# Two experts per row instead of eight: rows gathered by expert behind an attention layer

## The reference

```python
def xattn(latents, context, Wq, Wk, Wv, Wo):       # 16 heads, 4 key/value heads of 96
    hidden = concatenate([context, latents], axis=1)
    q, k, v = latents @ Wq.T, hidden @ Wk.T, hidden @ Wv.T     # by heads
    attn = softmax(q k^T / sqrt(96))
    return (attn v) @ Wo.T
def ffn(x, W_gate, b_gate, W_e, b_e):
    _, top_idx = top_k(x @ W_gate + b_gate, 2)
    y_all = relu(einsum('bsd,edh->bseh', x, W_e) + b_e)        # 8 experts
    return take_along_axis(y_all, top_idx[..., None], axis=2).mean(axis=2)
x = x + xattn(layernorm(x), ctx, Wq, Wk, Wv, Wo)
x = x + ffn(layernorm(x), W_gate, b_gate, W_e, b_e)
```

## Time and profile before

| | |
|---|---|
| median of 3 runs | 3558.59 us (3557.27 to 3558.87) |
| the profiled execution | 3555.37 us; its span from first to last instruction 3553.6 us |
| TensorE (PE) | 3503.6 us busy, 99% of the span, 22132 passes |
| VectorE (DVE) | 2121.9 us, 60% |
| ScalarE (ACT) | 1706.8 us, 48% |
| GpSimd (POOL) | 893.4 us, 25% |
| DMA | 262.34 MB, mean 74 GB/s |
| granted clock of TensorE | 0.996 of full speed over the span |
| chain that ended last, by its largest share | L1404 on TensorE, 8% |

### The profile page before, as it was taken

One profiled execution on the slowest core, in us unless ns is written; L12 is line 12 of the kernel. 1 busy time (PEld: TensorE's weight loads), 2 busy tenths in 40 slices (PEclk: granted clock), 3 DMA queues, 4 the chain that ended last, 5 costly groups with the idle time before them and its releaser, 6 DMA issues. The chain is left out here.

```text
span 3553.6 us, 65357 instructions
## 1 busy us (share of the span) xinstructions
PE 3503.6 (99%) x22132; PEld 3228.6 (91%) x22132; DVE 2121.9 (60%) x3055; ACT 1706.8 (48%) x3204; POOL 893.4 (25%) x692
## 2 busy tenths in 40 slices
PE   8999999999999999999999999999999999898999
PEld 8989999999999999999999999999999999887887
DVE  5356666666666666666666666666666666555554
ACT  3235555555555555555555555555555555423222
POOL 0042222222222222222222222222222222400000
PEclk9999999999999999999999999999999999999999
DMA  6532222222222222222222222222222222363110
GB/s 229 201 120 62 62 62 62 62 62 62 62 62 62 62 60 60 61 62 62 62 62 62 62 60 59 61 62 62 61 59 60 61 62 62 93 192 114 36 36 33
DMA packets 301138, 262.34 MB, mean 74 GB/s; under 512 B 198690, under 2 KB 255394, under 8 KB 300466
## 3 DMA queue, kind: packets, MB, share of 16 engines
q1 hardware_dynamic: 301106, 261.94, 24.9%
HBM read 195.50 MB, written 66.35 MB: 74 GB/s over the span
## 5 line engine op out<-in xcount | busy, mean ns | idle before, releaser
L812 PE MATMUL ps_proj<-wv_hi,parts 128*125 128x384 f32 x3072 | 875.1, 339 | 0.0
L757 DVE TENSOR_TENSOR probs_lo<-probs,probs_hi 125x448 fp32r<-125x448 f32 (+1 forms) x896 | 679.9, 775 | 275.5 <-ACT probs_hi L684 263.1
L799 PE MATMUL ps_proj<-parts,wk_hi 128*128 128x500 f32 x2304 | 709.7, 389 | 2.9 <-DVEq L712 2.9
L812 PEld LDWEIGHTS ps_proj<-wv_hi,parts 128*125 128x125 f32 x3072 | 560.0, 186 | 4.7
L676 ACT ACTIVATE probs<-ps_scores 125x448 f32<-125x448 f32 (+1 forms) x896 | 463.0, 517 | 116.4 <-PE ps_scores L860 73.4
L812 PE MATMUL ps_proj<-wv_lo,parts 128*125 128x384 f32 x1536 | 518.4, 337 | 0.0
L799 PEld LDWEIGHTS ps_proj<-parts,wk_hi 128*128 128x128 f32 x2304 | 430.7, 188 | 90.9 <-DVEq L712 3.2
L663 ACT CAST values_hi<-ps_proj 125x384 fp32r<-125x384 f32 x384 | 184.5, 480 | 661.9 <-PE ps_proj L812 661.9
L684 ACT CAST probs_hi<-probs 125x448 fp32r<-125x448 f32 (+1 forms) x896 | 484.1, 540 | 28.3
L134 POOL TENSOR_SCALAR parts<-raw 128x1000 fp32r<-128x1000 f32 (+1 forms) x198 | 239.4, 1209 | 968.8 <-PE ps_proj L812 790.2
L726 DVE TENSOR_TENSOR values_lo<-ps_proj,values_hi 125x384 fp32r<-125x384 f32 x384 | 214.2, 558 | 430.1 <-ACT values_hi L663 428.1
(11 more groups left out here) (159 smaller groups left out, 6115.0 us busy)
## 6 DMA issues: line engine op xcount, KB each, us to landing
raw<-in_ctx SPq DMA_DIRECT2D x192, 500.0 KB, 3.6
qk_hi<-proj_out_hi SPq DMA_DIRECT2D x60, 224.0 KB, 2.0
qk_lo<-proj_out_lo SPq DMA_DIRECT2D x60, 224.0 KB, 2.4
queries_hi<-qk_hi SPq DMA_DIRECT2D x32, 336.0 KB, 3.5
queries_lo<-qk_lo SPq DMA_DIRECT2D x32, 336.0 KB, 3.6
att_raw<-attended SPq DMA_DIRECT2D x128, 84.0 KB
probs<-att_raw SPq DMA_DIRECT2D x31, 336.0 KB, 5.6
probs<-inverse_sums SPq DMA_DIRECT2D x31, 336.0 KB, 3.0
```

The costliest lines, as they stand in the source:

```text
L757: dve.tensor_tensor(prs[1][0:R, u % PRING, 0:N], pr[0:R, u % PRING, 0:N], f(prs[0][0:R, u % PRING, 0:N]), ALU.subtract).then_inc(p_lo, 1)
L799: mm = pe.matmul(pproj[n % 2][:, 0:CS], w["wk"][a][:, j // 3, i * P:(i + 1) * P], ct[v][:, c, j // 3, :], start=(j == 0), stop=(j == 3 * K ...
L812: mm = pe.matmul(pproj[n % 2][0:VT, 0:KD], ct[a][:, t // VTC, j // 3, s], w["wv"][v][:, j // 3, :], start=(j == 0), stop=(j == 3 * KT - 1))
```

## The change

Each row goes to its two experts only. In **combine**, gate writes for each row two one-hot rows (`sels`) of the chosen experts. A matrix product with a triangle of ones counts, for each row, how many rows of its tile ahead of it chose the same expert, and one with a matrix of ones adds those of all tiles before (rank). VectorE's put makes of it a place in a list (expert x 1792 + rank), and GpSimd writes the row's number to that place in DRAM by an indirect DMA, two for each tile (scatter). GpSimd also splits five eighths of every expert's weights, and rows and normed rows are stored to DRAM untransposed.

In **experts**, a table of 35 tiles of 128 places is worked out: for each tile its expert and where its part of the list lies. 35 is the number that suffices for any choice of the experts; all 35 are always computed. The list is gathered (one indirect DMA), turned, and then for each tile GpSimd gathers 128 normed rows by their numbers; TensorE turns them, ScalarE and VectorE split them, and TensorE multiplies by the weights of the tile's expert, whose number it reads from SBUF into a register. One tile's product has 15 passes, as one of the four blocks of rows lies in two homes: nine of 512 columns and six of 256. VectorE adds the bias chosen by its own register, ScalarE applies relu and 0.5, SP stores the tile to DRAM. When all are stored, each tile of 128 rows gathers its two results by indirect DMA, and VectorE adds both to the rows.

In **attend**, the maxima are spread otherwise over the value tiles, and row_max, turn and place_max move.

The core of the diff:

```diff
+NT = (2 * ROWS + E * (P - 1)) // P
+EARLY_W, LATE_W = 2 * D + D // 2, D // 2 + D
+LATE_RING, LO_PIECES = 4, 4
+XRING, X1_RAW = 3, 6
+PIECES = ((0, 0, 0, 0, D), (1, 0, D, 0, D), (2, 0, 2 * D, 0, D // 2), (2, 1, 0, D // 2, D), (3, 1, D // 2, 0, D))
 def value_parts(t):
-    first = (CHUNKS - 1) * KTILES + 2 * t
-    return first, first + 1
+    first = (CHUNKS - 1) * KTILES
+    return (first + max(2 * t - 1, 0), first + 2 * t if 0 < t < READY - 1 else PARTS)
...
                         if t == READY - 1:
+                            row_max(b)
+                        if t == READY:
                             place_max(b)
                         values(b, t)
-                        if p < PARTS:
+                        if last < PARTS:
                             part_max(b, last)
-                        if last + 1 == PARTS:
-                            row_max(b)
...
-                        if t == READY - 1:
-                            turn_max(b)
+                            if (t, part) == (READY, 0):
+                                turn_max(b)
...
# combine, SP
+                def load_expert(e):
+                    if e >= 2:
+                        sp.wait_ge(e_lo, e - 1)
+                    sp.dma_start(w_raw[:, e % 2], io["we"][:, e, 0:EARLY_W]).then_inc(e_loaded[e % 2], 16)
+                def store_rows(t):
+                    sp.wait_ge(x1_done, t + 1)
+                    sp.dma_start(scratch["x1"][t], x1[:, t % 2]).then_inc(x1_stored[t % 2], 16)
+                    sp.wait_ge(normed, t + 1)
+                    sp.dma_start(scratch["xn"][t * P:(t + 1) * P], xn[:]).then_inc(xn_stored, 16)
...
# combine, GpSimd
+                def split_expert(e):
...
+                    pool.tensor_scalar(hi, raw, 1.0, 0.0, ALU.mult, ALU.add).then_inc(e_hi, 1)
+                    pool.wait_ge(e_hi, e + 1)
+                    n = EARLY_W // LO_PIECES
+                    for i in range(LO_PIECES):
+                        c = slice(i * n, (i + 1) * n)
+                        op = pool.tensor_tensor(lo[:, c], raw[:, c], f(hi[:, c]), ALU.subtract)
+                    op.then_inc(e_lo, 1)
+                def scatter(t):
+                    pool.wait_ge(placed, t + 1)
+                    for n in range(2):
+                        pool.indirect_dma_start(out=scratch["ids"], out_offset=bass.IndirectOffsetOnAxis(pos[:, t, n:n + 1], 0),
+                                                in_=ids[:, t:t + 1], in_offset=None).then_inc(scattered, 16)
...
# combine, VectorE: put(t - 2) stands ahead of gate(t - 1)
+                def put(t):
+                    dve.wait_ge(ranked, t + 1)
+                    dve.tensor_tensor(place[:], pr[:], base[:], ALU.add).then_inc(place_ready, 1)
...
+                    dve.tensor_copy(pos[:, t, :], spots[:, t, :]).then_inc(placed, 1)
+                    dve.tensor_tensor(cum[:], cum[:], tot[:], ALU.add).then_inc(cum_ready, 1)
# combine, TensorE: rank(t - 2) six passes before the end of output(t)
+                def rank(t):
+                    pe.wait_ge(tot_ready, t + 1)
+                    pe.matmul(pr[:], upper[:], tot[:], start=True, stop=False)
+                    pe.wait_ge(cum_ready, START + t)
+                    pe.matmul(pr[:], allones[:], cum[:], start=False, stop=True).then_inc(ranked, 1)
...
# experts, SP
+                for j in range(NT):
+                    sp.wait_ge(relu_done, j + 1)
+                    sp.dma_start(scratch["y"][j * P:(j + 1) * P], y[:, j % XRING]).then_inc(y_stored[j % XRING], 16)
...
# experts, GpSimd
+                pool.wait_ge(row_ready, 1)
+                pool.wait_ge(early["scattered"], 32 * OT)
+                pool.indirect_dma_start(out=id_rows[:], out_offset=None, in_=scratch["ids"].rearrange("(j p) c -> j (p c)", p=P),
+                                        in_offset=bass.IndirectOffsetOnAxis(id_row[:], 0)).then_inc(ids_loaded, 16)
+                pool.wait_ge(index_done, 1)
+                for j in range(NT):
+                    if j >= XRING:
+                        pool.wait_ge(turned, j - XRING + 1)
+                    pool.indirect_dma_start(out=xg[:, j % XRING], out_offset=None, in_=scratch["xn"],
+                                            in_offset=bass.IndirectOffsetOnAxis(index[:, j:j + 1], 0)).then_inc(gathered[j % XRING], 16)
...
+                for t in range(OT):
+                    s = t % XRING
+                    if t >= XRING:
+                        pool.wait_ge(added, t - XRING + 1)
+                    for n, dst in enumerate((xg[:, s], y[:, s])):
+                        pool.indirect_dma_start(out=dst, out_offset=None, in_=scratch["y"],
+                                                in_offset=bass.IndirectOffsetOnAxis(y_pos[:, t, n:n + 1], 0)).then_inc(y_gathered[s], 16)
# experts, VectorE
+                for j in range(NT):
+                    e = dve.value_load(expert_i[0:1, j:j + 1], min_val=0, max_val=E - 1)
+                    if j + 1 < NT:
+                        lo(j + 1)
...
+                    dve.tensor_tensor(y[:, s], po[s][:], bias[:, bass.ds(e, 1), :].rearrange("p e d -> p (e d)"), ALU.add).then_inc(biased, 1)
# experts, TensorE
+                def product(j, e):
+                    pe.wait_ge(x_lo, j + 1)
+                    if j >= XRING:
+                        pe.wait_ge(biased, j - XRING + 1)
+                    for i, (k, home, c, d0, d1) in enumerate(PIECES):
+                        w = (we_early, we_late)[home]
+                        for a, v in TERMS:
+                            mm = pe.matmul(po[j % XRING][:, d0:d1], xs[a][:, j % XRING, k, :],
+                                           w[v][:, bass.ds(e, 1), c:c + d1 - d0].rearrange("p e d -> p (e d)"),
...
+                for j in range(2):
+                    turn(j)
+                pe.wait_ge(early["late_lo"], E)
+                for j in range(NT):
+                    e = pe.value_load(expert_i[0:1, j:j + 1], min_val=0, max_val=E - 1)
+                    product(j, e)
+                    if j + 2 < NT:
+                        turn(j + 2)
```

More of the change, by code:

```diff
@@ new lines, in _ @@
+                invert_sums(dve, stream, B - 1)
+                split(1)
+                dve.wait_ge(b_hi, 1)
+                dve.tensor_tensor(be_lo.bitcast(F32R), be_raw, f(be[0:E, :]), ALU.subtract).then_inc(b_lo, 1)
+                dve.wait_ge(consts, 14)
+                for t in range(OT - 1):
+                    norm(t)
+                    if t + 2 < OT:
+                        split(t + 2)
+                    if t > 1:
+                        put(t - 2)
+                    if t > 0:
+                        gate(t - 1)
@@ L1162, in _ @@
+                put(OT - 3)
+                gate(OT - 2)
+                norm(OT - 1)
+                put(OT - 2)
+                gate(OT - 1)
+                put(OT - 1)
             @block.tensor
@@ new lines, in experts @@
+        of_j = sb("of_j", [1, NT, E], I32)
+        over, tiles = sb("over", [P, E, SLOTS]), sb("tiles", [P, E])
+        pairs, ends = sb("pairs", [P, E, E]), sb("ends", [P, E])
+        shift, moved, move = sb("shift", [P, E]), sb("moved", [P, 2 * OT, E]), sb("move", [P, 2 * OT])
+        y_pos = sb("y_places", [P, OT, 2], U32)
+        sels, spots, base = (early[n] for n in ("selected", "spots", "bases"))
+        past, before = (x1_more[0:1, 2 + i, 0:NT * E].rearrange("p (j e) -> p j e", e=E) for i in range(2))
@@ L1384, in _ @@
-                for s in range(2):
-                    tile(0, s, True, first=(s == 0))
-                with dve.Fori(1, OT // 2 - 1) as i:
-                    for s in range(2):
-                        tile(i, s, True)
-                for s in range(2):
-                    tile(OT // 2 - 1, s, s == 0)
+                dve.wait_ge(consts, 7)
+                dve.tensor_copy(pick[:], pick_f[:]).then_inc(consts, 1)
+                dve.wait_ge(counted, 1)
+                dve.tensor_tensor(over[:], pcnt.unsqueeze(2).broadcast_to([P, E, SLOTS]), of_m[:], ALU.is_gt).then_inc(table, 1)
@@ L1416, in _, with spread_bias, turn @@
-                for s in range(2):
-                    tile(0, s, first=(s == 0))
-                with pe.Fori(1, OT // 2) as i:
-                    for s in range(2):
-                        tile(i, s)
+                def spread_bias(n):
+                    if n >= 2:
+                        pe.wait_ge(bias_ready, n - 1)
+                    pe.matmul(pb[n % 2][:], pick[:, n, :], be[:], start=True, stop=True).then_inc(spread, 1)
+                def turn(j):
+                    pe.wait_ge(gathered[j % XRING], 16 * (j // XRING) + 16)
+                    if j >= 2:
+                        pe.wait_ge(x_lo, j - 1)
+                    for k in range(KT):
+                        mm = pe.transpose(pt[j % 2][:, k, :], xg[:, j % XRING, k * P:(k + 1) * P], ident[:])
+                    mm.then_inc(turned, 1)
@@ new lines, in _ @@
+                pe.wait_ge(early["cum_ready"], START + OT)
```

(9 more changed lines are left out.)

602 lines of the change are left out of this document (302 added, 300 removed).

## The result

The changed kernel takes 3432.13 us (median of 4 runs, 3431.87 to 3433.05) against 3558.73 us for the kernel before on the same chip; the ratio is 0.9644, with a 95% interval of 0.9627 to 0.9661. The forecast was 3445, in a range of 3405 to 3520. The profiled execution has a span of 3430.3 us, 123.3 less than before.

A forecast was written before the change was run, and what follows sets the result against it. TensorE was taken to bound both long stages. Attend -14.0, combine +11.9 and last stage -109.2 (211.6 against 320.8) took the span from 3553.6 to 3442.3; 1.8 around it made 3444.1, stated as 3445 us, range 3405 to 3520.

The forecast's parts named there:

- the signs that I had named for being wrong: Prediction wrong if an indirect DMA's issue on GpSimd exceeds 2 us or the list tiles' pitch exceeds 4.5 us.
- Part 1: Attend: moved maxima remove a 0.48 us gap per batch (15.4 us), new wait costs 1.4; net -14.0 us (-18 to -8).
- Part 2: Combine: rank and a gate in the stream, longer tail, GpSimd's splits delaying VectorE 3.3 us; sum +11.9 us.
- Part 3: Start of the last stage: a chain ahead of the first product, then passes at low clock; 23.1 us, bounds 18 and 33.
- the issue c: GpSimd's issue of one indirect DMA, at the last stage's start and in its gathers; taken as 1.3 us.
- Part 4: Last stage's 35 list tiles at 3.9 us each, 0.6 of it for register addresses; 136.5 us (115 to 190).
- Part 5: Results gathered back behind the last product, 13 pairs at 2.9 us plus both ends; 52.0 us (40 to 75).
- the addresses: Rival, list tiles: TensorE's register addresses cost more, pitch 5.5 instead of 3.9 us, adding 56, total 3500; chance 0.16.
- the descriptors: Rival, last stage: indirect DMA issues take 2.8 us as software writes 128 rows; +42 us, total 3487; chance 0.15.
- the slow case: Rival, combine and last stage: indirect DMA issues above some 4.15 us cancel the gain; 3575 at 4.4 us; chance 0.05.
- GpSimd's block: Rival, combine: GpSimd's split pieces block VectorE for all 24 us, total 3466; chance 0.04.
- movement and descriptors are both cheap: Rival, last stage: 768 KB moves in 2.2 us and issues take 0.9 us; total 3434; chance 0.05.

The follow-up runs named there:

- e5_scatter_later: Changed kernel with the last tile's two scatters issued in the last stage, behind GpSimd's constants, not in combine; 3426.00 us.
- e3_lo_first: Changed kernel with VectorE's first four late lo parts moved from behind the row numbers to the head of its last-stage program; 3428.38 us.
- e2_fixed_expert: Changed kernel with list tile j's expert fixed at j modulo 8, so no register addresses on TensorE or VectorE; 3431.03 us.
- e10: Changed kernel with six buffers, not three, for each of a tile's two gathered results behind the last product; 3429.61 us.
- e11: Changed kernel with six result buffers, the second result read plainly by SyncE and not gathered; 3422.00 us.
- e12_best: Changed kernel with the last stage's start reordered, last scatters later, and results scattered beside the products, then read plainly, not gathered; 3409.57 us.

## Why the prediction held, step by step

The forecast time is 13 us off, and that it is no more is in part luck: three parts came out 3.3, 5.7 and 5.1 us longer than forecast and two shorter, one by 23.2. Of the signs that I had named for being wrong, an issue above 2 us came in one place (the row numbers) and the pitch stayed below 4.5.

- **Part 1, -14.0 (-18 to -8): -10.7, and -10.1 with the edit alone.** The gap of 0.48 us went as said. The new wait is 0.13 us per batch, 4.2 us, where I took 1.4; it lay within the bound of 6.4.
- **Part 2, +11.9: +17.6.** Tiles 10.5 us apart, as said. In the stream, 13.1 where I took 10.9, the stalls are 1.41 (the second tile's output, for a lo part of VectorE) and 2.74, and the half clock behind the second costs 1.5: 5.7 us where I took 3.3. GpSimd's pieces were met, but in one tile. That the stores "stay covered" was wrong there: the DMA engines were full (1.06) and norm waited 3.74 us for one. The larger miss is the tail: +1.0 forecast, measured 4.4 (17.6 - 13.2). I left out that a barrier right behind scatters passes 4.1 us later than their last issue ends, which e5_scatter_later took away. The Trainium skill's rule (SBUF — State Buffer, "Who interferes with whom") agrees with the length of each block, 2.88 us behind an operation of 2.88; its 24 us bound did not come.
- **Part 3, 23.1: 28.2** (the terms ahead of the low clock add up to 20.7, where I wrote 20.8; measured 25.7 to the first product, and 5.31 us for that one where later ones take 2.80: granted clock 0.50, 1.2 GHz, after 25.7 us in which TensorE was busy for 8.3). The term that failed is the issue c for the row numbers: 1.3 forecast, 4.39 measured, with a landing 7.6 behind its start in the place of 4.1. e3_lo_first names the cause. The Trainium skill's 2.0 us plus bytes at 436 GB/s (DMA: Bandwidth & Descriptors, "Anatomy of one DMA") comes near that run's row numbers, 2.4 us, and not near the gathers of the last part, which land 4.6 to 4.8 us behind their issue; these have other transfers beside them, with the DMA engines at 0.73.
- **Part 4, 136.5 (115 to 190): 113.3,** 35 x 3.237 (turns from 3270.58 to 3374.16, 32 pitches), below the low bound. The mis-sized term is 0.6 us per tile for register addresses: nothing, by e2_fixed_expert. The products themselves I had at 3.3. This alone is -23.2 and more than the whole miss of 12 to 13 us.
- **Part 5, 52.0: 49.9.** c is 1.25 where I took 1.3. I had the pair at 2.9 us, between issue and movement; it is 2.74, and it is the issues (e10 and e11).

The sum of the misses, 3.3 + 5.7 + 5.1 - 23.2 - 2.1 = -11.2, less 0.8 since the last two list tiles have no turn, makes 3432.1 of 3444.1; the profiled execution has 3430.3 + 1.8 = 3432.1. Of the rivals, the addresses are refuted; the descriptors cost more only where an issue met such operations of VectorE, above all at the start, and so for another reason than software writing 128 rows; the slow case needed c above 4.15 in every issue; GpSimd's block is real, with 1.8 us of its 24 (1.54 and 0.78 in the place of 0.36 and 0.17). The low rival "movement and descriptors are both cheap" would have had c at 0.9: the engine's own 0.95 came near it, but the 0.30 between two issues makes 1.25.

## What to carry to other kernels

An indirect DMA of 128 rows costs GpSimd 1.25 us, be it of 4 or of 2048 bytes a row, so put it where GpSimd idles under a long TensorE stage; here a scatter beside the products replaced 28 gathers at the end and took 15 us off it (49.9 to 35.0). Keep two-input VectorE operations away from the moment at which an indirect DMA is issued, and don't end a stage with one. When halving a suspected bound changes nothing, look for a second one just below before the first is acquitted: with three buffers the gathers looked innocent, with six they were the bound.

## What the runs showed of the hardware that I had not expected

- An issue of an indirect DMA beside an operation of VectorE with two inputs in SBUF ends about 1 us behind the end of that operation (1.75 and 1.39 us in the changed kernel), or behind the whole row of four (4.39, 5.00, 3.55 and 4.98 us in four kernels); in e3_lo_first, with none of the four beside it, it takes 1.04. Among the list tiles, where VectorE's operations have one input in PSUM, the 32 gathers issued from 3264 on take 0.94 or 0.95, and in e12_best the scatters right beside such an operation 0.96 to 1.00. The Trainium skill's page SBUF — State Buffer, "Who interferes with whom", infers that such an operation does not hold descriptor generation, as it takes only the read side of the shared ports. In these runs the issue of an indirect DMA is held all the same; whether its descriptors wait or its reading of the row numbers, which also lie in SBUF, no run tells apart. Why it is one operation at some times and all four at others I have not settled.
- A barrier right behind an indirect DMA passes 3.5 to 4.2 us behind the end of its issue, and 0.28 us (e5_scatter_later) and 0.29 us (e12_best) behind VectorE's last operation where the last scatters come later. Scatters of 128 single numbers were through 3.6 to 5.6 us behind the end of their issue.
- A wait of TensorE can cost more than its length: behind the 2.74 us of the second tile the granted clock was 0.51 for 3.4 us, another 1.5 us; behind 2.79 us in e3_lo_first and 2.21 in e2_fixed_expert it stayed at 1.00.
- An address from a register in a TensorE operand costs nothing that can be seen at passes of 0.12 to 0.23 us, whereas SyncE's issues with one leave 0.27 us.
